# Four graph-attention layers on one core: the second half's destination tiles divided 5 + 3 instead of 6 + 2

## The chip, the core and the metric

The kernel runs on one NeuronCore of a Trainium2 chip. The metric is the device time of one execution in microseconds (us); the kernel is compared by the median of several executions. Engines are called by the profile's names: PE is TensorE (PEld its weight loads), DVE VectorE, ACT ScalarE, SP SyncE, POOL GpSimd.

## The reference

2048 nodes with 128 features each, in float32, pass through four layers `x = x + gnn(relu(layernorm(x)))` under one adjacency matrix. Layer 0 has eight heads; layers 1 to 3 have one. A head computes, for nodes n (destinations) and m (sources):

```
Wh = h @ W;   s1 = Wh @ a1;   s2 = Wh @ a2
e[n, m]  = leaky_relu(s1[n] + s2[m], 0.2), masked where adj[n, m] == 0
att      = softmax over m of e
out[n]   = act(att @ Wh)      # elu; exact gelu in layer 1; the heads of layer 0 are joined and go through W_out
```

## The kernel before

**Tiles and passes.** The 2048 nodes are 16 tiles of 128. The weights of the softmax are built transposed, 128 sources by up to 1024 destinations, by one VectorE instruction per source tile (`late_probs`, L1166; L1070 for the heads of layer 0 before the last half), and land in `probs`, a ring of eight slots of 1024 columns. TensorE takes them as stationary operand and multiplies them with `V` (129 columns: 128 features and one of factors, whose sum is the denominator), adding up over 16 source tiles in PSUM. One such matmul in float32 shows as two records. The destinations of a pass are `groups(p)`, each a group of 129 columns in `acc`; three groups fit a bank of 512.

The destinations of a layer are taken in three passes p = 0, 1, 2, numbered by `PARTS`: pass 0 has the first half (eight tiles), pass 1 six tiles of the second half, pass 2 the last two. In this text pass 1 is called the second pass and pass 2 the last pass. Each entry of `PARTS[p]` is a chunk of (first tile, count), in which the work behind a pass is done: denominators (`late_denominators`), division or activation from PSUM (`late_divide`, or `nonlinear_late` on ScalarE), ELU or GELU, the add to the node rows `X` (`add_linear`, `add_to_x`), statistics (`late_moments`, `late_variance`), inverse root (ScalarE's `late_inverse_root` and VectorE's `late_scale`; in layer 1's output for passes 0 and 1 Newton steps on VectorE alone), normalised rows (`late_norm` on VectorE, `late_normed` on ScalarE, shared out by `NORM_DVE`), transposes on TensorE (`transpose_normed`), ReLU into `hT` (`late_relu`, L834), and the next layer's `Wh` and scores (`late_wh`, L483). Layer 0 also has a transpose and a projection of its last head's rows (`transpose_rows`, `project_rows`).

**The seam.** A new layer can start its first pass only when the scores of all 16 tiles are there: `take_scores` reads the score columns from PSUM, the maximum over all of them is spread to all partitions by a matmul (`spread_late_max`, L497), `late_center` subtracts it, and `late_factors` and `exponent_rows` make the factors that the first `late_probs` needs.

**The order** on each engine is written out by hand, and an engine runs its instructions in that order, waiting on semaphores. On TensorE work of other kinds stands inside a pass at a place (j, half): behind the first half of the groups of source tile j (half 0), or behind all (half 1). In the layers' main sequence on VectorE (from L1363 on) the calls `tiles(n, p, first, end)` build source tiles; before, all sixteen of the last pass stand directly behind those of the second pass, and the second pass's denominators follow them. For the last pass four source tiles share one slot of the ring (256 columns each), and VectorE waits for a slot once for four. In layers 0 and 2 the last pass's `late_denominators` and `late_divide` stand, on VectorE, ahead of part of the second pass's work (`late_moments(1, 1)`; `late_norm(3, 1)`). On ScalarE `late_inverse_root` of the last pass stands ahead of the second pass's `late_relu` in layer 1 (both chunks) and in layer 2 (its second chunk).

Of the kernel before, what the change touches and what calls it, by code (L numbers as in the profile page):

```python
# [14 lines left out]
def gat_stack(nc, x, adj_t, w0, w0_t, a0, w_out, b_out, w1_t, w1, r1, w2, w2_t, av2, w3, w3_t, av3, out):  # L15
# [5 lines left out]
    N, D = x.shape  # L21
    H = w0.shape[0]
    P = 128
# [16 lines left out]
    PARTS = (((0, 4), (4, 4)), ((0, 4), (4, 2)), ((6, 2),))  # L40
    FIRST, CHUNKS = (0, 2, 4), 5
    NORM_DVE = ((0, 0), (1, 1), (2,))

    ctx = ExitStack()
    with ctx:
# [43 lines left out]
        late_part = sb("late_part", [P, 1])  # L89
# [24 lines left out]
        warm_bank, spare_bank, max_bank = acc[:, 1, 0, 0:P], acc[:, 0, 2, 0:2 * P], acc[:, 0, 2, 2 * P:3 * P]  # L114
# [96 lines left out]

        def group(c, k):

            return acc[:, c, k // PER_BANK, (k % PER_BANK) * VW:(k % PER_BANK) * VW + VW]
# [50 lines left out]
        def slot_no(n, p, j):  # L265

            return NT * (2 * H - 2) + (2 * NT + NT // 4) * n + NT * p + (j // 4 if p == 2 else j)
# [3 lines left out]
        def slot_of(n, p, j):  # L271

            at = (j % 4) * width(p) if p == 2 else 0
            return probs[:, slot_no(n, p, j) % RING, at:at + width(p)]
# [56 lines left out]
        def _(pe):  # L331
# [61 lines left out]
            def unit(u, c, q, asides=()):  # L393

                for j in range(NT):
# [10 lines left out]
                    for k in range(NK):  # L406
                        if first and k == NK // 2:
                            pe.wait_ge(probs_ready, 1)
                        last = nc.tensor.matmul(group(c, k), probs[:, j % RING, k * P:(k + 1) * P], V[:, j, :],  # L409
                                                start=(j == 0 and k % PER_BANK == 0), stop=(j == NT - 1),  # L410
# [6 lines left out]
            def late_unit(n, p, asides):  # L417

                c, v = half_of(p), V_of[n % 2]
                for j in range(NT):  # L420
# [8 lines left out]
                    for i, k in enumerate(groups(p)):  # L429
                        if p == 0 and j == 0 and k == NK // 2:  # L430
                            pe.wait_ge(probs_ready, tile_no(n, p, j) + 1)
                        last = nc.tensor.matmul(group(c, k), slot_of(n, p, j)[:, i * P:(i + 1) * P], v[:, j, :],  # L432
                                                start=(j == 0 and k % PER_BANK == 0), stop=(j == NT - 1),
# [134 lines left out]
            def rest_of_scores(n):  # L568
# [10 lines left out]
                else:  # L579
# [7 lines left out]
                late_s1(n, 2, hT_ready, chunk_no(n, 1, 0))  # L587
# [10 lines left out]
            late_unit(0, 2, {(9, 1): lambda: transpose_rows(1, 0, hT_ready, 1),  # L598
                             (10, 1): lambda: transpose_rows(1, 1, hT_ready, 2),
                             (11, 1): lambda: project_rows(1, 0),  # L600
                             (13, 0): lambda: project_rows(1, 1)})
# [368 lines left out]
        def _(dve):  # L970
# [54 lines left out]
            def last_columns(to, c):  # L1025

                full = NK // PER_BANK
                nc.vector.tensor_copy(to[:, 0:full * PER_BANK].rearrange("p (b g) -> p b g", g=PER_BANK),
                                      acc[:, c, 0:full, D:D + PER_BANK * VW - D:VW])
                link(nc.vector.tensor_copy(to[:, full * PER_BANK:NK],  # L1030
                                           acc[:, c, full, D:D + (NK - full * PER_BANK - 1) * VW + 1:VW]))
# [137 lines left out]
            def tiles(n, p, first, end):  # L1169

                for j in range(first, end):
# [4 lines left out]
                    if p < 2 or j % 4 == 0:  # L1176
# [11 lines left out]
            def late_denominators(n, p):  # L1188
# [3 lines left out]
                whole = 2 * PER_BANK  # L1192
# [326 lines left out]
```

## Time and profile before

| | |
|---|---|
| median of 3 runs | 776.5 us (775.86 to 779.19) |
| the profiled execution's own time | 776.41 us |
| its span (first to last instruction) | 774.7 us |
| mean granted TensorE clock | 0.988 of full speed |
| PE busy | 750.0 us (97%) |
| DVE busy | 626.4 us (81%) |
| ACT busy | 328.8 us (42%) |
| seam 1, layer 0 to 1: end of the last pass, first matmul of the next pass | 551.8 us, 567.8 us |
| seam 2, layer 1 to 2 | 627.9 us, 641.6 us |
| seam 3, layer 2 to 3 | 702.0 us, 712.6 us |
| end of the last pass of layer 3 | 770.5 us |

Times inside the execution are microseconds from the start of the span. A busy TensorE is counted from records whose ends are modelled, so the start of a record says more than its end. In the chain of work that ended last each piece was released by the one ahead of it; where the chain stays on one line of TensorE, nothing else holds the kernel up. In a timeline several instructions of a kind are merged into one row, with their number at the end and, in brackets, the idle time of the engine ahead of them.

### The profile page before, as it was taken

Reading aid. Unit: us, or ns where it says so; the run is one execution under the profiler, and the core shown is the slowest. Engines: PE = TensorE matmul, PEld = TensorE weight load, DVE = VectorE, ACT = ScalarE, POOL = GpSimd, SP = SyncE. Lnnn points to the kernel's source line nnn. Section 1 sums busy time; section 2 is a strip of 40 time slices with the busy share of each in tenths; the row PEclk is TensorE's granted clock in tenths of the full one; section 3 lists DMA queues with packets and bytes.
Section 4 is the critical chain, followed back from the end, with each engine's and each line's share of the span. In section 5 each row is a group of like instructions: output and inputs, shape, how many; then the busy total and the mean of one; then the engine's idle time right before and its main releaser. Section 6 shows DMA issues by size and latency. Waiting matters only on the chain.

```text
span 774.7 us, 15961 instructions
## 1 busy us (share of the span) xinstructions
PE 750.0 (97%) x6451; PEld 731.0 (94%) x6451; DVE 626.4 (81%) x1042; ACT 328.8 (42%) x888; POOL 16.1 (2%) x36
## 2 busy tenths in 40 slices
PE   8899899999999999999999999999889989998997
PEld 7699799999999999999999999999789969996997
DVE  4896788797877978879788796888588949997986
ACT  5875562343543246134354334623441244535420
POOL 3000000000000000000000000000000000000000
PEclk9999999999999999999999999999999989999999
DMA  9794000000000000000000000000000000000001
GB/s 298 269 364 159 28 2 28 27 0 27 2 25 27 0 27 0 27 27 0 27 17 10 27 0 27 0 0 2 0 2 1 1 1 1 2 1 1 1 19 38
DMA packets 13874, 29.39 MB, mean 38 GB/s; under 512 B 1296, under 2 KB 7568, under 8 KB 13840
## 3 DMA queue, kind: packets, MB, share of 16 engines
q1 hardware_dynamic: 11152, 20.00, 7.6%
q0 software_dynamic: 2688, 8.92, 3.4%
q8 instruction: 24, 0.39, 0.2%
q14 instruction: 10, 0.08, 0.0%
HBM read 27.80 MB, written 1.11 MB: 37 GB/s over the span
## 4 chain that ended last, share of the span: by engine, by line
PE 85%; ACT 5%; DMA 4%; DVE 4%; issue 1%; SPq 0%; DVEq 0%; ACTq 0%
PE acc L409 49%; PE acc L432 25%; DMA stage<-in_adj_t_dram 4%; PE side L509 3%; PE side L365 3%; PE acc L483 2%; ACT adjT L623 1%; DVE probs L1070 1%; ACT hpT L716 1%; DMA W0t<-in_W_t_dram 1%; PE side L471 1%; ACT hT L834 0%; PE side L457 0%; PE side L491 0%; ACT xn L825 0%
## 5 line engine op out<-in xcount | busy, mean ns | idle before, releaser
L409 PE MATMUL acc<-V,probs 128*128 128x129 f32 x3840 | 438.1, 276 | 1.9 <-DVE probs L1064 1.9
L409 PEld LDWEIGHTS acc<-V,probs 128*128 128x128 f32 x3840 | 434.0, 192 | 4.9 <-ACT V L657 2.7
L1070 DVE SCALAR_TENSOR_TENSOR probs<-rho,t_now,adjT 128x1024 f32<-128x1024 f32 x224 | 272.9, 1277 | 11.4 <-PE acc L409 9.1
L1166 DVE SCALAR_TENSOR_TENSOR probs<-rho,t_now,adjT 128x768 f32<-128x768 f32 (+3 forms) x179 | 146.7, 880 | 9.6 <-PE acc L432 6.6
L716 ACT ACTIVATE hpT<-rows 32x256 f32<-32x256 f32 x224 | 92.8, 414 | 71.1 <-DVE rows L1107 68.6
L432 PEld LDWEIGHTS acc<-stage,probs 128*128 128x128 f32 x1024 | 115.0, 192 | 4.0 <-ACT stage L865 3.7
L432 PE MATMUL acc<-stage,probs 128*128 128x129 f32 x1024 | 116.1, 275 | 2.1 <-DVE probs L1166 2.1
L432 PE MATMUL acc<-V,probs 128*128 128x129 f32 x768 | 89.4, 275 | 0.0
L432 PEld LDWEIGHTS acc<-V,probs 128*128 128x128 f32 x768 | 87.4, 192 | 1.0 <-ACT V L865 0.9
L1115 DVE TENSOR_TENSOR X<-X,side 128x512 f32<-128x512 f32 x28 | 19.3, 688 | 65.0 <-PE side L509 65.0
L701 ACT ACTIVATE fill<-mean_now,empty 128x128 f32<-128x128 f32 x112 | 34.2, 397 | 87.9 <-DVE den L1083 87.9
L679 ACT ACTIVATE V<-v_now 128x4 f32<-128x4 f32 x28 | 5.9, 209 | 82.2 <-PE side L365 82.2
L1092 DVE SCALAR_TENSOR_TENSOR rows<-acc,den,fill 128x128 f32<-128x128 f32 x112 | 30.9, 343 | 7.1 <-ACT fill L701 6.8
L623 ACT ACTIVATE adjT<-stage 128x1024 bf16<-128x1024 int32 x32 | 33.0, 1052 | 8.5 <-DMA stage<-in_adj_t_dram 8.4
L509 PE MATMUL side<-Wout,hpT 128*128 x224 | 28.9, 285 | 3.8 <-ACT hpT L716 3.8
L681 ACT ACTIVATE V<-side,v_now 128x128 f32<-128x128 f32 x112 | 31.4, 362 | 0.0
L509 PEld LDWEIGHTS side<-Wout,hpT 128*128 128x128 f32 x224 | 27.7, 202 | 4.0 <-issue 4.0
L365 PE MATMUL side<-W,hT 128*128 x224 | 29.6, 275 | 0.0
L365 PEld LDWEIGHTS side<-W,hT 128*128 128x128 f32 x224 | 27.3, 192 | 0.0
L800 ACT ACTIVATE rows<-acc,late_den 128x128 f32<-128x128 f32 x32 | 11.0, 398 | 36.4 <-DVE late_den L1203 21.6
L825 ACT ACTIVATE xn<-X,nwt 128x128 f32<-128x128 f32 x36 | 14.6, 481 | 18.5 <-DVE nwt L1304 18.5
L708 ACT ACTIVATE rows<-rows 128x512 f32<-128x512 f32 x28 | 17.7, 631 | 10.9 <-DVE rows L1092 10.7
(190 smaller groups left out, 416.6 us busy)
## 6 DMA issues: line engine op xcount, KB each, us to landing
stage<-in_adj_t_dram SPq DMA_DIRECT2D x32, 512.0 KB, 7.0
rho<-rho_dram POOLq DMA_DIRECT2D x15, 512.0 KB, 3.9
X<-in_x_dram SPq DMA_DIRECT2D x2, 512.0 KB, 4.4
W0t<-in_W_t_dram SPq DMA_DIRECT2D x1, 512.0 KB, 5.1
W<-in_L_gnn_W_heads_dram SPq DMA_DIRECT2D x1, 512.0 KB, 6.4
Wout<-in_L_gnn_W_out_dram POOLq DMA_DIRECT2D x1, 512.0 KB, 10.4
out_dram<-X SPq DMA_DIRECT2D x1, 512.0 KB, 3.7
out_dram<-X SPq DMA_DIRECT2D x1, 384.0 KB, 3.0
```

The costliest lines, as they stand in the source:

```text
L365: last = nc.tensor.matmul(side[:, g % 2, k * D:(k + 1) * D], hT[:, j * P:(j + 1) * P], w, start=True, stop=True)
L409: last = nc.tensor.matmul(group(c, k), probs[:, j % RING, k * P:(k + 1) * P], V[:, j, :], start=(j == 0 and k % PER_BANK == 0), stop=(j == ...
L432: last = nc.tensor.matmul(group(c, k), slot_of(n, p, j)[:, i * P:(i + 1) * P], v[:, j, :], start=(j == 0 and k % PER_BANK == 0), stop=(j = ...
L509: last = nc.tensor.matmul(side[:, b, k * D:(k + 1) * D], hpT[:, 4 * b + k, :], w, start=True, stop=True)
L623: nc.scalar.activation(adjT[:, j, c * CH:(c + 1) * CH], stage[:, n % STAGE, :], ACT.Sign).then_inc(adj_ready, 1)
L681: last = nc.scalar.activation(V[:, 4 * g + k, 0:D], side[:, g % 2, k * D:(k + 1) * D], ACT.Copy, scale=v_now[:, 4 * g + k:4 * g + k + 1])
L701: ins = nc.scalar.activation(fill[:, k, :], mean_now[:, :], ACT.Copy, scale=empty[:, c, k:k + 1])
L716: last = nc.scalar.activation(hpT[b:b + Q, :, a:a + Q], rows[a:a + Q, 1, :, b:b + Q], ACT.Copy)
L1070: nc.vector.scalar_tensor_tensor(probs[:, j % RING, :], rho[:, c * CH:(c + 1) * CH], t_now[:, j:j + 1], adjT[:, j, c * CH:(c + 1) * CH], A ...
L1092: ins = nc.vector.scalar_tensor_tensor(rows[:, 0, k, :], group(c, k)[:, 0:D], den[:, 3, k:k + 1], fill[:, k, :], ALU.mult, ALU.add)
L1115: nc.vector.tensor_tensor(at, at, side[:, b, :].rearrange("p (k d) -> p k d", k=4), ALU.add).then_inc(x_added, 1)
L1166: return nc.vector.scalar_tensor_tensor(slot_of(n, p, j)[:, first:end], rho[:, at + first:at + end], t_now[:, j:j + 1], adjT[:, j, at + fi ...
```

## The change

`PARTS` divides the second half 5 + 3 instead of 6 + 2: the second pass has tiles 0 to 4 in chunks of 3 and 2, the last pass tiles 5 to 7 in one chunk. The banks of the second half hold 3, 2 and 3 groups (`BANKS`, `place`, `last_of_bank`), so that each bank belongs to one pass. `spare_bank`, where the last pass's chunk is transposed, is three tiles wide. A slot of the ring holds two source tiles of the last pass (384 columns each) instead of four (`PER_SLOT`). VectorE builds source tiles 0 to 11 of the last pass ahead of the second pass's denominators and 12 to 15 behind them (and behind the divisions, where there are any). In layer 0's last pass, `transpose_rows` and `project_rows` stand at source tiles 6 to 9 instead of 9 to 13. `late_denominators`, `last_columns` and `take_scores` read the denominators or scores bank by bank; the maximum of the scores is one reduction over all 16 columns behind the last copy, where before a partial maximum was joined with the last two columns straight from PSUM. `NORM_DVE` gives all three of the last pass's normalised tiles to VectorE, as both were before.

```diff
@@ -37,9 +37,11 @@
     ALPHA, EPS = 0.2, 1e-5
-    PARTS = (((0, 4), (4, 4)), ((0, 4), (4, 2)), ((6, 2),))
+    PARTS = (((0, 4), (4, 4)), ((0, 3), (3, 2)), ((5, 3),))
+    BANKS = ((0, 3, 6, 8), (0, 3, 5, 8))
+    PER_SLOT = 2
     FIRST, CHUNKS = (0, 2, 4), 5
-    NORM_DVE = ((0, 0), (1, 1), (2,))
+    NORM_DVE = ((0, 0), (1, 1), (3,))
@@ -86,7 +88,6 @@
         late_max = sb("late_max", [P, 1])
-        late_part = sb("late_part", [P, 1])
@@ -111,7 +112,7 @@
         first_xn = [xn, rows[:, 0, :, :]]
-        warm_bank, spare_bank, max_bank = acc[:, 1, 0, 0:P], acc[:, 0, 2, 0:2 * P], acc[:, 0, 2, 2 * P:3 * P]
+        warm_bank, spare_bank, max_bank = acc[:, 1, 0, 0:P], acc[:, 0, 2, 0:3 * P], acc[:, 0, 2, 3 * P:4 * P]
@@ -209,9 +210,19 @@
+        def place(c, k):
+            b = max(b for b in range(NB) if BANKS[c][b] <= k)
+            return b, k - BANKS[c][b]
+        def last_of_bank(c, b):
+            return acc[:, c, b, D:D + (BANKS[c][b + 1] - BANKS[c][b] - 1) * VW + 1:VW]
-            return acc[:, c, k // PER_BANK, (k % PER_BANK) * VW:(k % PER_BANK) * VW + VW]
+            b, at = place(c, k)
+            return acc[:, c, b, at * VW:at * VW + VW]
@@ -264,13 +275,13 @@
-            return NT * (2 * H - 2) + (2 * NT + NT // 4) * n + NT * p + (j // 4 if p == 2 else j)
+            return NT * (2 * H - 2) + (2 * NT + NT // PER_SLOT) * n + NT * p + (j // PER_SLOT if p == 2 else j)
-            at = (j % 4) * width(p) if p == 2 else 0
+            at = (j % PER_SLOT) * width(p) if p == 2 else 0
@@ -407,7 +418,7 @@
                         last = nc.tensor.matmul(group(c, k), probs[:, j % RING, k * P:(k + 1) * P], V[:, j, :],
-                                                start=(j == 0 and k % PER_BANK == 0), stop=(j == NT - 1),
+                                                start=(j == 0 and place(c, k)[1] == 0), stop=(j == NT - 1),
@@ -430,7 +441,7 @@
                         last = nc.tensor.matmul(group(c, k), slot_of(n, p, j)[:, i * P:(i + 1) * P], v[:, j, :],
-                                                start=(j == 0 and k % PER_BANK == 0), stop=(j == NT - 1),
+                                                start=(j == 0 and place(c, k)[1] == 0), stop=(j == NT - 1),
@@ -584,7 +595,7 @@
                 spread_late_max(n)
-                late_s1(n, 2, hT_ready, chunk_no(n, 1, 0))
+                late_s1(n, 2, hT_ready, chunk_no(n, 1, 1))
@@ -595,10 +606,10 @@
                              **scores_of_half(1, 15)})
-            late_unit(0, 2, {(9, 1): lambda: transpose_rows(1, 0, hT_ready, 1),
-                             (10, 1): lambda: transpose_rows(1, 1, hT_ready, 2),
-                             (11, 1): lambda: project_rows(1, 0),
-                             (13, 0): lambda: project_rows(1, 1)})
+            late_unit(0, 2, {(6, 0): lambda: transpose_rows(1, 0, hT_ready, 1),
+                             (7, 0): lambda: transpose_rows(1, 1, hT_ready, 2),
+                             (8, 0): lambda: project_rows(1, 0),
+                             (9, 0): lambda: project_rows(1, 1)})
@@ -1024,11 +1035,14 @@
-                full = NK // PER_BANK
-                nc.vector.tensor_copy(to[:, 0:full * PER_BANK].rearrange("p (b g) -> p b g", g=PER_BANK),
-                                      acc[:, c, 0:full, D:D + PER_BANK * VW - D:VW])
-                link(nc.vector.tensor_copy(to[:, full * PER_BANK:NK],
-                                           acc[:, c, full, D:D + (NK - full * PER_BANK - 1) * VW + 1:VW]))
+                if c == 0:
+                    full = NK // PER_BANK
+                    nc.vector.tensor_copy(to[:, 0:full * PER_BANK].rearrange("p (b g) -> p b g", g=PER_BANK),
+                                          acc[:, c, 0:full, D:D + PER_BANK * VW - D:VW])
+                else:
+                    for b in range(2):
+                        nc.vector.tensor_copy(to[:, BANKS[1][b]:BANKS[1][b + 1]], last_of_bank(1, b))
+                link(nc.vector.tensor_copy(to[:, BANKS[c][2]:NK], last_of_bank(c, 2)))
@@ -1173,7 +1187,7 @@
                         dve.wait_ge(late_rho_ready, 4 * n)
-                    if p < 2 or j % 4 == 0:
+                    if p < 2 or j % PER_SLOT == 0:
@@ -1189,16 +1203,8 @@
                 dve.wait_ge(summed, tile_no(n - 1, p, NT))
-                whole = 2 * PER_BANK
-                steps_of = ([(0, whole)] if ks[0] == 0 else []) + ([(whole, NK)] if ks[-1] == NK - 1 else [])
-                for k0, k1 in steps_of:
-                    if k0 == 0:
-                        src = acc[:, c, 0:2, D:D + PER_BANK * VW - D:VW]
-                    else:
-                        src = acc[:, c, 2, D:D + (k1 - k0 - 1) * VW + 1:VW]
-                    to = late_den[:, c, 2 if n == 2 else 1, k0:k1]
-                    if k0 == 0:
-                        to = to.rearrange("p (b g) -> p b g", g=PER_BANK)
+                for b in (range(NB) if p == 0 else (0, 1) if p == 1 else (2,)):
+                    src, to = last_of_bank(c, b), late_den[:, c, 2 if n == 2 else 1, BANKS[c][b]:BANKS[c][b + 1]]
@@ -1316,20 +1322,16 @@
-                whole = 2 * PER_BANK
                 dve.wait_ge(late_wh_psum, stage_no(n, p))
-                if p == 1:
-                    link(nc.vector.tensor_copy(scores[:, NK:NK + whole].rearrange("p (b g) -> p b g", g=PER_BANK),
-                                               acc[:, 1, 0:2, D:D + PER_BANK * VW - D:VW]))
-                    link(nc.vector.tensor_reduce(late_part[:, :], scores[:, 0:NK + whole], AX.X, ALU.max))
-                else:
-                    nc.vector.scalar_tensor_tensor(late_max[:, :], acc[:, 1, 2, D:D + 1], acc[:, 1, 2, VW + D:VW + D + 1],
-                                                   late_part[:, :], ALU.max, ALU.max).then_inc(late_max_ready, 1)
-                    link(nc.vector.tensor_copy(scores[:, NK + whole:NT], acc[:, 1, 2, D:D + (NK - whole - 1) * VW + 1:VW]))
+                for b in ((0, 1) if p == 1 else (2,)):
+                    last = nc.vector.tensor_copy(scores[:, NK + BANKS[1][b]:NK + BANKS[1][b + 1]], last_of_bank(1, b))
+                link(last)
+                if p == 2:
+                    nc.vector.tensor_reduce(late_max[:, :], scores[:, :], AX.X, ALU.max).then_inc(late_max_ready, 1)
@@ -1372,10 +1374,11 @@
             tiles(0, 1, 14, 16)
-            tiles(0, 2, 0, 16)
+            tiles(0, 2, 0, 12)
             late_divide(1, 1, 1)
+            tiles(0, 2, 12, 16)
@@ -1422,8 +1425,9 @@
                     tiles(1, 1, 13, 16)
-                    tiles(1, 2, 0, 16)
+                    tiles(1, 2, 0, 12)
                     late_denominators(2, 1)
+                    tiles(1, 2, 12, 16)
@@ -1446,10 +1450,11 @@
                     tiles(2, 1, 15, 16)
-                    tiles(2, 2, 0, 16)
+                    tiles(2, 2, 0, 12)
                     late_divide(3, 1, 1)
+                    tiles(2, 2, 12, 16)
@@ -1473,10 +1478,11 @@
                     tiles(3, 1, 14, 16)
-                    tiles(3, 2, 0, 16)
+                    tiles(3, 2, 0, 12)
                     late_divide(4, 1, 1)
+                    tiles(3, 2, 12, 16)
```

## Rows read from the trace of the kernel before

**Rows 1.** The page, the chain that ended last: shares of the span by line.

```profile
PE acc L409 49%; PE acc L432 25%; DMA stage<-in_adj_t_dram 4%; PE side L509 3%; PE side L365 3%; PE acc L483 2%; ACT adjT L623 1%; DVE probs L1070 1%; ACT hpT L716 1%; DMA W0t<-in_W_t_dram 1%; PE side L471 1%; ACT hT L834 0%; PE side L457 0%; PE side L491 0%; ACT xn L825 0%
```

**Rows 2.** The chain by time (start, us, what, records), layer 2, last pass.

```profile
694.83 7.15 PE acc L432 x64
```

**Rows 3.** The timeline (start, us, engine, line, operation, shapes, count): VectorE's passes.

```profile
533.20 8.27 DVE L1166 SCALAR_TENSOR_TENSOR probs<-rho,t_now,adjT 128x768 f32<-128x768 f32 x18
...
685.52 7.35 DVE L1166 SCALAR_TENSOR_TENSOR probs<-rho,t_now,adjT 128x768 f32<-128x768 f32 x17
```

**Rows 4.** The timeline, layer 0: second pass and last pass.

```profile
528.66 0.69 DVE L1255 TENSOR_TENSOR X<-X,side 128x512 f32<-128x512 f32 x1 [0.88 <-PE side L457]
...
533.31 3.19 ACT L825 ACTIVATE xn<-X,nwt 128x128 f32<-128x128 f32 x8 [1.04 <-DVE nwt L1304]
...
536.50 0.60 PE L471 MATMUL side<-ident,xn 128*128 128x128 f32 x4
...
541.82 0.17 DVE L1205 TENSOR_SCALAR late_den<-acc 128x6 f32<-128x6 f32 x1 [0.34 <-PE acc L432]
...
542.24 1.64 DVE L1221 SCALAR_TENSOR_TENSOR rows<-acc,late_den,fill 128x128 f32<-128x128 f32 x6
...
544.87 0.69 DVE L1231 SCALAR_TENSOR_TENSOR rows<-rows 128x512 f32<-128x512 f32 x1
...
546.97 0.60 PE L449 MATMUL side<-ident,rows 128*128 128x128 f32 x4
```

**Rows 5.** The timeline, seam between layers 0 and 1.

```profile
552.25 0.61 DVE L1221 SCALAR_TENSOR_TENSOR rows<-acc,late_den,fill 128x128 f32<-128x128 f32 x2
...
552.77 1.25 DVE L1269 BATCH_NORM_STATS2 stats<-X 128x6 f32<-128x128 f32 x6
...
560.08 0.29 ACT L811 ACTIVATE nwt<-mv,eps_col 128x2 f32<-128x2 f32 x1
...
562.49 0.38 PE L471 MATMUL acc<-ident,xn 128*128 128x128 f32 x2
...
564.55 0.49 PE L497 MATMUL acc<-ident,late_max 128*128 128x128 f32 x2 [0.40 <-DVE late_max L1330]
```

**Rows 6.** The timeline, second pass of layer 2: normalised rows and their transposes.

```profile
685.64 3.19 ACT L825 ACTIVATE xn<-X,nwt 128x128 f32<-128x128 f32 x8 [1.97 <-DVE nwt L1304]
...
688.66 0.60 PE L471 MATMUL side<-ident,xn 128*128 128x128 f32 x4
```

**Rows 7.** The timeline, seam between layers 1 and 2.

```profile
630.07 0.60 ACT L800 ACTIVATE rows<-acc,late_den 128x128 f32<-128x128 f32 x2
...
632.42 0.58 ACT L834 ACTIVATE hT<-side 128x512 f32<-128x512 f32 x1
...
635.09 0.63 PE L471 MATMUL acc<-ident,xn 128*128 128x128 f32 x2
...
637.91 0.80 PE L497 MATMUL acc<-ident,late_max 128*128 128x128 f32 x2 [0.40 <-DVE late_max L1330]
```

**Rows 8.** The timeline, seam between layers 2 and 3.

```profile
703.60 0.60 DVE L1313 TENSOR_SCALAR xn<-X,mv,nwt 128x128 f32<-128x128 f32 x2
...
705.37 0.29 ACT L811 ACTIVATE nwt<-mv,eps_col 128x2 f32<-128x2 f32 x1
...
709.36 0.49 PE L497 MATMUL acc<-ident,late_max 128*128 128x128 f32 x2 [0.40 <-DVE late_max L1330]
```

**Rows 9.** Windows: stretch, length, busy us by engine (PE first), PEclk, DMA, GB/s.

```profile
557.00:559.00 2.00, 0.54 (x5) 0.57 (x6) 1.59 (x8) 1.65 (x4) 0.00 (x0) 0.98 0.00 0
...
559.00:561.00 2.00, 1.65 (x8) 1.25 (x7) 0.32 (x2) 1.44 (x6) 0.00 (x0) 0.50 0.00 0
...
634.00:636.00 2.00, 1.72 (x9) 1.32 (x7) 0.33 (x2) 0.24 (x1) 0.00 (x0) 0.51 0.00 0
```

**Rows 10.** DMA issues: count, KB each, us from issue to landing.

```profile
out_dram<-X SPq DMA_DIRECT2D x1, 384.0 KB, 3.0
...
out_dram<-X SPq DMA_DIRECT2D x1, 128.0 KB, 1.8
```

## The prediction

> **What bounds the kernel now.** The first view is the page's chain of work that ended last, by line: the two matmul lines of the attention passes (L409, L432) carry 49% and 25% of the span [rows 1]. TensorE is therefore the bound wherever passes run, and the change leaves the number of matmuls as it is. The second view is the same chain in order of time, from 515 us on: inside a pass it is a single run of L432, the last pass of a layer being 64 matmul records in 7.15 us, 0.1117 us each [rows 2], two records for one fp32 matmul, so 0.223 us for one tile of destinations. Between the last matmul of a layer and the first of the next the chain breaks into small pieces on VectorE, ScalarE and TensorE: three seams (their bounds stand in the table of the profile) and a tail. So I read the timeline there, asking for each seam which of two strands ends last: the one of the second pass (destinations 8 and up) or that of the last pass.
>
> **The passes.** Per source tile the second pass takes five matmuls instead of six and the last pass three instead of two: 16 x (5+3) is 16 x (6+2). TensorE's sum is unchanged, but the second pass ends 16 x 0.223 = 3.57 us earlier. For VectorE the two longest runs of L1166 differ by one 768-wide instruction, 8.27 - 7.35 = 0.92 us; the rest of the shorter run is sixteen 256-wide ones, 6.43 us, 0.402 each [rows 3]. The line through both (0.518 us for 512 columns) is 0.14 us + 1.01 ns per column: 0.79 us for 640 columns, 0.53 us for 384. I take that slope for every other instruction that gets wider too: +0.13 us for 128 columns. Sum per source tile 1.32 us as before. The ring is what shifts: two last-pass tiles share a slot now instead of four, so the last four wait for tiles 14 and 15 of the second pass, and stand behind the second pass's denominators and divisions. They start at the latest 2 us after the second pass's end and TensorE wants tile 12 only 12 x 0.67 = 8 us into the last pass: no cost for TensorE, but 4 x 0.53 = 2.1 us more ahead of everything that VectorE does next for the second pass.
>
> **Where TensorE may now stand inside a pass.** TensorE gets earlier by 0.22 us per second-pass tile, VectorE by only 0.13, so work that TensorE takes from the other engines in mid-pass loses slack.
> - Layer 0, second pass. The add to X behind the projection at tile 7 (528.66) comes 8 x 0.223 = 1.79 us earlier, one 768-wide tile then saves 0.13: the normalised rows of ScalarE are 1.92 us earlier. TensorE wants them at tile 13, 14 x 0.223 = 3.13 us earlier. Of eight instructions in 3.19 us four are done after 1.65, so ready was 533.31+1.65+0.14 (semaphore) = 535.10 against 536.50 [rows 4]: slack 1.40 goes to 0.19. No cost.
> - Layer 0, last pass. VectorE is through with its asides at 533.20-1.92 = 531.28; two tiles and twelve of the last pass (1.58+6.38) end at 539.24, while the second pass, whose denominators began at 541.82, ends 3.57 earlier, at 538.2. Denominators 0.42, five divisions at 0.26 (six and two of them take 1.64 and 0.61, [rows 4, 5]), four tiles 2.1 and the first ELU (0.4+0.55 at 384 columns) make its rows ready at 544.15 with the semaphore; before they were at 545.56 with TensorE there at 546.97 [rows 4]. The transposes stood behind ten tiles, so the last pass began at 546.97 - 10x0.447 = 542.50, and now begins at 538.93; their new place, inside tile 6 behind one of three, comes at 538.93 + 6x0.67 + 0.22 = 543.17. TensorE stands 1.0 us. The second chunk (tile 7) is then in time. One tile less in this transposing and projecting gives 0.33 back: the pass ends 0.65 later.
> - Layer 2, second pass. By the same count the normalised rows are 1.04 + 3 x 0.13 = 1.43 us earlier (VectorE's tile 11 starts when second-pass tile 3 is done, four tiles of 0.22, and is itself 0.13 shorter), TensorE 3.13 us: 685.64+1.65+0.14 = 687.43 against 688.66 [rows 6] is slack 1.23, and becomes -0.47. Cost **0.5 us**.
> - Layers 1 and 3: no such point ends late by this count.
>
> **Seam 1 (layer 0 to 1).** Here VectorE keeps its order: denominators of the last pass, its divisions, and only then the statistics of the second pass. So its strand starts with the last matmul and the 3.57 us of cover buy nothing. The divisions gain one (+0.26), the ELU and its transposes are wider (+0.2, +0.1, copy +0.1); one statistic less is -0.2 (six took 1.25). ScalarE's root of the last part (560.08) is queued behind the copy of the transposed second-pass rows: with 0.65 from the pass I put it at 560.70. The add to X, statistics and norm of three instead of two (+0.13, +0.26, +0.26) overlap with that wait but for the norm: ready for TensorE at 562.8. Before, the transposes began at 562.49, and it was TensorE that was late, coming from a stretch with a clock of 0.50 [rows 5, 9]. Transpose +0.11, relu +0.11, two matmul records more +0.22, scores +0.15 (copy and then maximum, where one instruction of 0.22 did both): the spread of the maximum (564.55, [rows 5]) comes at 565.5. **+1.0 us**, the wait in the pass included.
>
> **Seam 2.** The one seam where the second pass's strand is late: its statistics and the Newton steps end only after the last matmul, so ScalarE comes to the last pass's GELU at 630.07 and, past a table load and the root, to the second pass's relu at 632.42 [rows 7]. With 3.57 us more cover, less the 2.1 us of tiles, this strand is out of the way, and the GELU starts on the last denominators, 0.4 us behind the last matmul, at 628.35. From GELU to relu took 2.35 us; a third tile adds 0.6 (division or GELU 0.26, add 0.07 to 0.13, statistics 0.26): relu at 631.3, 1.1 earlier. From here the clock decides. It was 0.51 in 634 to 636 [rows 9], and the transposes at 635.09 waited for TensorE's own slow matmuls. If it stays at 2.4 GHz, the norm sets them, at 633.0, and 2.06 for the way to the spread with 0.6 for the third tile gives 635.7 instead of 637.91, with 0.3 more behind it: -2.5. If it falls before 632, the third tile eats the gain: -0.2. From transpose to spread took 2.82 at the low and 2.06 at the high clock [rows 5, 7]. I take **-1.5**, a little nearer to the fast end, since TensorE's idle stretch ahead of the relu shrinks by that 1.1 us.
>
> **Seam 3.** The second pass's strand was ready before the last matmul except for VectorE's two norms (703.60), which stand behind denominators, divisions and an add of the last pass, and they stay there. VectorE is one serial chain: +0.26 division, +0.13 and +0.13 for two adds to X, +0.26 statistics, so the root at 705.37 moves to 706.15; norm +0.26, transpose and relu +0.22, matmuls +0.22, scores +0.15 up to the spread (709.36) [rows 8]. **+1.6 us.** The second chunk's relu waits behind that root on ScalarE, inside the same stretch. Nothing is late next.
>
> **Tail.** Division and two adds of 384 columns: +0.5; the last store is 192 KB instead of 128: between 1.8 and 3.0 us for 128 and 384 KB [rows 10], +0.3. **+0.8 us.** Two more copies of last columns per denominator lie under TensorE's passes; where VectorE sets a wait they add 0.1 in all.
>
> **Sum.** 1.0 + 0.5 - 1.5 + 1.6 + 0.8 + 0.1 = +2.5 us on the profiled execution (776.41 us, span 774.7), which is the median of 776.5 to 0.1. So **779.0 us**, +0.3%. About 0.5% (3.9 us) is what a measurement of this kernel can tell from no change.
>
> **Rivals.**
> - *The cover works everywhere.* VectorE is ahead enough that TensorE doesn't stand in the passes (-0.5, and seam 1 without its 1.0), and seam 2 brings its full 2.5: 1.6+0.8+0.1-2.5 = 0.0, 776.5 us. For it: slacks of 0.2 to 1 us rest on a straight line between two widths. Against: two separate waits would have to be absent.
> - *The clock, slower.* In seam 3 TensorE's holes grow: behind the first three second-pass matmuls about 0.9 us, behind the last two 0.7, where before it had nearly none. Before seam 1's drop its busy time was 0.54 of 2 us [rows 9]; I count about 0.8 to 1.0 of 2 here. If it falls, transpose to spread is 0.76 longer [rows 5, 7] and the second-pass matmuls some 0.4; with seam 2 at -0.2 the sum is 1.0+0.5-0.2+1.6+0.8+0.1+1.2 = +5.0, 781.5 us. It decides if the granted clock is at its low level anywhere in the first 9 us of seam 3. The Trainium skill (TensorE: Matmul & The Clock Gate, "What's actually happening") says that the throttled state is the default and activity releases it; by that rule a seam that grew idler is the place to fall. This trace agrees in two seams of three.
> - *The cover is not used in seam 2 either* (another engine's order holds it): 1.0+0.5+1.6+0.8+0.1 = +4.0, 780.5 us.
>
> **Chances.** Forecast 0.40, cover everywhere 0.25, cover unused 0.11, clock 0.17, a gain I don't see 0.07. Slower by over 0.5%: the clock and half of the unused cover, 0.23; faster 0.07; within 0.70. The range takes in 776.5 and 781.5 with the few tenths by which executions differ: 775.8 to 781.9.
>
> **What would show it.** In the profile after: layer 0's transposes in the last pass with some 1 us of idle TensorE before them; VectorE's last four tiles right behind the divisions; GELU of the last part at about 0.4 us behind the last matmul in seam 2, relu some 1 us earlier; in seam 3 the root 0.8 us further behind the last pass's denominators; a tail 0.8 us longer. The forecast is wrong if seam 3 is not longer, or if seam 2's gain is not near 1 to 2 us.

## Result, and the profile after

The changed kernel takes 779.36 us (median of 20 runs, 777.66 to 781.76), the kernel before 776.88 (20 runs, 773.91 to 779.19); the ratio is 1.0033, 95% interval 1.0022 to 1.0044. The medians differ by 2.5 us (2.6 by the ratio), which is below the 0.5% that was called no change, and clear of zero. The profiled execution of the changed kernel took 777.76 us, near the fastest of its twenty.

The page of the kernel after: its span, TensorE's busy time and the chain by line. Line numbers are 11 higher on TensorE and ScalarE: L443 is L432 of before, L482 is L471, L494 L483, L502 L491, L508 L497, L811 L800, L822 L811, L836 L825, L845 L834.

```profile
span 776.1 us, 15973 instructions
...
PE 749.7 (97%) x6451; PEld 730.7 (94%) x6451; DVE 627.5 (81%) x1060; ACT 328.1 (42%) x885; POOL 16.1 (2%) x36
...
PE acc L420 50%; PE acc L443 23%; DMA stage<-in_adj_t_dram 4%; PE side L520 3%; PE side L376 3%; DVE probs L1180 2%; PE acc L494 1%; ACT adjT L634 1%; PE acc L390 1%; ACT hpT L727 1%; DVE stats L1275 1%; DVE rows L1227 0%; PE side L502 0%; ACT hT L845 0%; PE side L468 0%
```

TensorE is busy for 749.7 us instead of 750.0: the work is the same, and the chain has lost 2% at the pass line (L443 23%, L432 25% [rows 1]) to VectorE (L1180, L1275, L1227). That share is the length of the chain on VectorE ahead of two points where TensorE now waits for it, in layer 0 and in layer 2; it is not the length of the waits. To see how long they are, I cut both profiled executions at TensorE's own marks: the first matmul of layer 0's second pass, the first score matmul behind each last pass (L491, now L502), and the matmul for the mean (L389, now L400), which stands inside the first pass of layers 2 and 3.

| stretch, us | before | after | difference | forecast |
|---|---|---|---|---|
| layer 0, second and last pass | 36.58 | 37.30 | +0.72 | +0.65 |
| seam 1 and layer 1 | 76.28 | 76.76 | +0.48 | +0.35 |
| seam 2 to the mean of layer 2 | 28.12 | 25.65 | -2.47 | -1.5 |
| layer 2 to the end of its last pass | 45.77 | 46.27 | +0.50 | +0.5 |
| seam 3 to the mean of layer 3 | 25.37 | 27.18 | +1.81 | +1.6 |
| layer 3 and the tail | 47.55 | 48.32 | +0.77 | +0.8 |
| sum | 259.67 | 261.48 | +1.81 | +2.5 (0.1 for the copies in it) |

(The heads of layer 0 ahead of this took 0.46 us less in the execution after, 514.61 us against 515.07; more of that below. Where times of layer 0 and seam 1 are compared with those of before, these 0.46 us have to be added.)

Layer 0, the timeline after (start us, us, engine, line, operation, shapes, count, idle before and its end):

```profile
538.75 0.22 DVE L1211 TENSOR_SCALAR late_den<-acc 128x3 f32<-128x3 f32 x2
...
540.54 2.20 DVE L1180 SCALAR_TENSOR_TENSOR probs<-rho,t_now,adjT 128x384 f32<-128x384 f32 x4
...
543.04 0.56 DVE L1237 SCALAR_TENSOR_TENSOR rows<-rows 128x384 f32<-128x384 f32 x1
...
543.75 0.52 PE L460 MATMUL side<-ident,rows 128*128 128x128 f32 x3 [0.87 <-DVE rows L1237]
...
560.22 0.29 ACT L822 ACTIVATE nwt<-mv,eps_col 128x3 f32<-128x3 f32 x1
...
562.38 0.85 PE L482 MATMUL acc<-ident,xn 128*128 128x128 f32 x3
...
565.37 0.49 PE L508 MATMUL acc<-ident,late_max 128*128 128x128 f32 x2 [0.53 <-DVE late_max L1334]
```

The second pass's denominators come at 538.75, three microseconds ahead of 541.82 [rows 4] (2.6 when the earlier start is taken off); the last four tiles (540.54) stand behind the divisions, the ELU behind them, and TensorE waits 0.87 us for it at 543.75. In seam 1 the last part's transposes begin at 562.38 and the spread comes at 565.37. With the 0.46 us added that is 562.84 and 565.83, 0.35 and 1.28 us later than before [rows 5] (forecast: 562.8 and 565.5). TensorE's clock falls in this seam as it did before: the three transposes take 0.85 us, where e5, whose clock stays high, takes 0.52 for them, starts them the same 10.5 us behind the pass's end, and reaches the spread 0.33 us sooner. In the window 560 to 562 the granted clock is at its low level:

```profile
560.00:562.00 2.00, 1.98 (x9) 1.98 (x10) 1.11 (x6) 0.72 (x4) 0.00 (x0) 0.50 0.00 0
```

Seam 2, the timeline, and two windows of it (columns as in [rows 9], the granted clock third from the right):

```profile
629.09 0.88 ACT L811 ACTIVATE rows<-acc,late_den 128x128 f32<-128x128 f32 x3 [2.75 <-DVE late_den L1209]
...
632.10 0.47 ACT L845 ACTIVATE hT<-side 128x384 f32<-128x384 f32 x1
...
633.93 0.49 PE L482 MATMUL acc<-ident,xn 128*128 128x128 f32 x3
...
636.56 0.49 PE L508 MATMUL acc<-ident,late_max 128*128 128x128 f32 x2 [0.53 <-DVE late_max L1334]
```

```profile
633.00:635.00 2.00, 1.43 (x13) 1.19 (x12) 0.91 (x5) 1.05 (x5) 0.00 (x0) 1.00 0.01 4
...
635.00:637.00 2.00, 1.38 (x9) 1.19 (x10) 0.33 (x2) 0.53 (x2) 0.00 (x0) 1.00 0.00 0
```

The last pass ends at 628.67 here, at 627.93 before. Counted from there, the last part's GELU starts after 0.4 us where it was 2.1; the relu comes after 3.4 us, 4.5 before [rows 7]; the clock stays at its high level, where it was 0.51 [rows 9].

Layer 2's second pass, seam 3 and the tail, the timeline; then a window behind the spread of seam 3, and the last store (count, KB, us to landing):

```profile
682.48 3.19 ACT L836 ACTIVATE xn<-X,nwt 128x128 f32<-128x128 f32 x8 [1.70 <-DVE nwt L1310]
...
684.27 0.63 PE L482 MATMUL side<-ident,xn 128*128 128x128 f32 x4 [0.31 <-ACT xn L836]
...
702.77 0.60 DVE L1319 TENSOR_SCALAR xn<-X,mv,nwt 128x128 f32<-128x128 f32 x2
...
704.94 0.30 ACT L822 ACTIVATE nwt<-mv,eps_col 128x3 f32<-128x3 f32 x1 [0.58 <-DVE mv L1281]
...
709.75 0.72 PE L508 MATMUL acc<-ident,late_max 128*128 128x128 f32 x2 [0.53 <-DVE late_max L1334]
...
771.08 0.16 DVE L1211 TENSOR_SCALAR late_den<-acc 128x3 f32<-128x3 f32 x1 [4.88 <-PE acc L443]
```

```profile
711.00:713.00 2.00, 2.00 (x4) 0.67 (x2) 1.59 (x4) 1.83 (x7) 0.00 (x0) 0.50 0.00 0
```

```profile
out_dram<-X SPq DMA_DIRECT2D x1, 192.0 KB, 2.1
```

TensorE waits for ScalarE's normalised rows at 684.27, which is 1.65 + 0.14 us behind their start, as counted for before [rows 6]. In seam 3 the last pass's denominators come at 700.79; before, they came at 702.02, and those of the tail at 770.49:

```profile
702.02 0.16 DVE L1205 TENSOR_SCALAR late_den<-acc 128x2 f32<-128x2 f32 x1 [0.64 <-PE acc L432]
...
770.49 0.16 DVE L1205 TENSOR_SCALAR late_den<-acc 128x2 f32<-128x2 f32 x1 [2.96 <-PE acc L432]
```

From these denominators to the root it is 4.15 us instead of 3.35 [rows 8], to the spread 8.96 instead of 7.34. In seam 3 the clock falls only about the spread (0.50 in 711 to 713). From the denominators to the end of the span the tail takes 5.0 us instead of 4.2.

### The profile page after: what moved, and what is told of

It is laid out like the page before. It is cut to its first block, busy times and chain, and to the rows that moved or that the text cites. A ratio compares the mean times of both kernels' runs of the same rounds, so it can differ in the third digit from the quotient of the medians.

```text
span 776.1 us, 15973 instructions
## 1 busy us (share of the span) xinstructions
PE 749.7 (97%) x6451; PEld 730.7 (94%) x6451; DVE 627.5 (81%) x1060; ACT 328.1 (42%) x885; POOL 16.1 (2%) x36
## 4 chain that ended last, share of the span: by engine, by line
PE 84%; DVE 7%; ACT 4%; DMA 4%; issue 1%; POOL 0%; DVEq 0%; ACTq 0%; POOLq 0%
PE acc L420 50%; PE acc L443 23%; DMA stage<-in_adj_t_dram 4%; PE side L520 3%; PE side L376 3%; DVE probs L1180 2%; PE acc L494 1%; ACT adjT L634 1%; PE acc L390 1%; ACT hpT L727 1%; DVE stats L1275 1%; DVE rows L1227 0%; PE side L502 0%; ACT hT L845 0%; PE side L468 0%
## 5 line engine op out<-in xcount | busy, mean ns | idle before, releaser
L1180 DVE SCALAR_TENSOR_TENSOR probs<-rho,t_now,adjT 128x640 f32<-128x640 f32 (+3 forms) x179 | 146.9, 878 | 12.3 <-PE acc L443 8.4
L443 PEld LDWEIGHTS acc<-stage,probs 128*128 128x128 f32 x1024 | 115.1, 192 | 2.8 <-ACT stage L876 2.6
L443 PE MATMUL acc<-stage,probs 128*128 128x129 f32 x1024 | 115.8, 275 | 1.0 <-DVE probs L1180 1.0
L443 PE MATMUL acc<-V,probs 128*128 128x129 f32 x768 | 89.4, 275 | 1.0 <-DVE probs L1180 1.0
L443 PEld LDWEIGHTS acc<-V,probs 128*128 128x128 f32 x768 | 87.4, 192 | 1.9 <-ACT V L876 1.8
L811 ACT ACTIVATE rows<-acc,late_den 128x128 f32<-128x128 f32 x32 | 11.1, 398 | 39.0 <-DVE late_den L1209 24.2
L719 ACT ACTIVATE rows<-rows 128x512 f32<-128x512 f32 x28 | 17.7, 630 | 10.6 <-DVE rows L1106 10.5
L836 ACT ACTIVATE xn<-X,nwt 128x128 f32<-128x128 f32 x33 | 13.5, 482 | 16.8 <-DVE nwt L1310 16.8
```

Of the source, the lines that this page charges most:

```text
L1180: return nc.vector.scalar_tensor_tensor(slot_of(n, p, j)[:, first:end], rho[:, at + first:at + end], t_now[:, j:j + 1], adjT[:, j, at + fi ...
```

## Experiments

Each is compared with the kernel before on the same chip in 10 to 12 runs, and by its profile with the same marks as above. A profile shows a stretch to 0.1 us; the ratios of the medians don't, their intervals are 0.3 to 0.4% wide. e5 to e8 ran on another chip than e1 to e4, so only ratios and stretches are compared between the two groups.

### e1: layer 0's asides two source tiles later

```diff
-            late_unit(0, 2, {(6, 0): transpose_rows(1, 0, ..), (7, 0): transpose_rows(1, 1, ..),
-                             (8, 0): project_rows(1, 0), (9, 0): project_rows(1, 1)})
+            late_unit(0, 2, {(8, 0): transpose_rows(1, 0, ..), (9, 0): transpose_rows(1, 1, ..),
+                             (10, 0): project_rows(1, 0), (11, 0): project_rows(1, 1)})
```

> The changed kernel with the four asides of layer 0's last pass (transposes and projection of the second pass's rows) two source tiles later: tiles 8, 9, 10 and 11 instead of 6, 7, 8 and 9. My theory: TensorE waits 0.87 us at tile 6 for VectorE's ELU, because VectorE comes to the second pass's denominators late and builds four more tiles first; two tiles later (1.34 us) the rows are there. Expected: no idle TensorE ahead of the transposes, the last pass of layer 0 ends 0.9 us earlier, the adds to X still well before it ends, the rest unchanged: 0.9 us less than the changed kernel, ratio to the kernel before about 1.002. Rival, the wait is no loss since TensorE waits elsewhere for it: the last pass ends at the same time, ratio 1.003.

Measured: 777.16 us, ratio 1.0017 (1.0003 to 1.0032). Layer 0's two passes take 36.25 us, 1.05 less than in the changed kernel and even 0.33 less than before, as forecast from the one tile that is projected behind the pass instead of in it. The transposes, in e1's timeline, have no idle time before them:

```profile
543.52 0.56 DVE L1237 SCALAR_TENSOR_TENSOR rows<-rows 128x384 f32<-128x384 f32 x1
...
544.52 0.49 PE L460 MATMUL side<-ident,rows 128*128 128x128 f32 x3
```

Seam 1 and layer 1 stay as they were (76.67 against 76.76). So the wait was a real loss of TensorE's time, and it depends on where the asides stand in the pass: with the same split, two source tiles later it is gone.

### e2: the second pass's strand ahead of the last pass's denominators

```diff
+            late_statistics(1, 1)
+            late_scale(1, 1)
+            late_norm(1, 1)
             late_denominators(1, 2)
             late_divide(1, 2, 0)
-            late_moments(1, 1)
             late_elu_rows(2, 0)
-            late_variance(1, 1)
-            late_scale(1, 1)
-            late_norm(1, 1)
...
+                    late_norm(3, 1)
                     late_denominators(3, 2)
                     late_divide(3, 2, 0)
                     add_linear(3, 2, 0)
-                    late_norm(3, 1)
```

and on ScalarE `late_inverse_root(1, 1)` and `late_normed(1, 1)` ahead of `late_exp_rows(1, 2, 0)`, and the second part of `late_normed(3, 1)` ahead of `late_exp_rows(3, 2, 0)`.

> The changed kernel with the second pass's strand taken out from behind the last pass's denominators where it stood behind them. In layer 0 statistics, scale and norm of the second pass stand ahead of the last pass's denominators on VectorE, and root and normalised rows ahead of the last pass's exponentials on ScalarE; in layer 2 the two norms of the second pass stand ahead of the last pass's denominators. My theory, the longer cover was bought and left unused there by the order: from the end of the last pass to the spread of the maximum seam 1 shrinks by about 1.7 us and seam 3 by 0.5; in all 2.2 us less than the changed kernel, ratio about 1.000 to 1.001. Rival, the strand of the last pass alone (its ELU, projection, statistics, norm) binds both seams whatever stands beside it: less than 0.5 us in all, ratio 1.003.

Measured: 777.95 us, ratio 1.0028 (1.0009 to 1.0047), where 1.000 to 1.001 was expected; the median does not tell e2 from the changed kernel. Past layer 0's heads its profile takes 260.40 us, 1.1 less than the changed kernel's 261.48 and not the 2.2 expected. From the end of the last pass to the spread, seam 1 is 1.04 us shorter (12.42 against 13.46), seam 3 0.51 (8.65 against 9.16). Seam 1 fell short of 1.7 for a reason its own timeline shows:

```profile
561.18 0.52 PE L482 MATMUL acc<-ident,xn 128*128 128x128 f32 x3 [1.47 <-DVE xn L1318]
...
562.37 1.66 PE L494 MATMUL acc<-WL,hT 128*128 128x129 f32 x6 [0.67 <-ACT hT L845]
...
564.55 0.79 PE L508 MATMUL acc<-ident,late_max 128*128 128x128 f32 x2 [0.53 <-DVE late_max L1333]
...
565.14 3.62 PE L502 MATMUL side<-hT,waL 128*128 128x512 f32 x4
```

The transposes came 1.4 us sooner behind the pass's end (9.05 us against 10.47). But TensorE, through with the second pass's work earlier, idled 1.47 us ahead of them. In the changed kernel the clock had fallen with the second pass's matmuls and was high again at the spread; now it fell behind the transposes and stayed low past the spread (0.50 in 566 to 568): six records that take 0.94 took 1.66, the four behind the spread 3.62 instead of 1.88. Of the 1.04 us at the spread only 0.2 are left at the next layer's first matmul. So VectorE's order did hold the cover back, as the theory has it; the clock took most of that gain again in seam 1.

### e3: the same order with 6 + 2

The diff is that of e2, on the kernel before.

> The kernel before (6 + 2) with the same change of order as in e2. My theory: with 6 + 2 the second pass's strand in layer 0 is not finished when the last pass ends (its last add to X ends 0.7 us ahead of the end), so putting it first delays the last pass's denominators by about 3 us and takes about as much out of the strand behind them: seam 1 within 1 us of the kernel before, either way; in seam 3 the two norms (0.5 us) fit ahead of the end: seam 3 shorter by 0.4. Ratio 0.999 to 1.001. Rival, the order alone is worth as much without the new split: ratio 0.997, as far below the kernel before as e2 is below the changed kernel.

Measured: 776.57 us, ratio 1.001 (0.999 to 1.0029). Seam 1 and layer 1 take 76.51 us (+0.23), seam 3 24.85 to the mean (-0.52). A row of its timeline, whose last pass ends at 551.97: the last pass's denominators, which came 0.2 us behind the pass in the kernel before, now wait for the second pass's statistics and norm.

```profile
555.11 0.15 DVE L1204 TENSOR_SCALAR late_den<-acc 128x2 f32<-128x2 f32 x1
```

The denominators come 3 us later, as expected, and seam 1 does not gain. In layer 0 the order needs the longer cover of 5 + 3; in seam 3 it does not.

### e4: seam 2 of the kernel before, with TensorE kept active

```diff
                     transpose_normed(n, 1, 1, hT_ready, chunk_no(n, 0, 1))
+                    if n == 2:
+                        keep_warm(9, warm_bank)
```

> The kernel before with nine matmuls of the identity on TensorE in seam 2, between the transposes of the second pass and the matmuls for the scores, where TensorE idles 2.4 us. They hold nothing up; they keep TensorE active. It measures what part of seam 2's gain in the changed kernel (2.5 us in the two profiles) is the clock and what the earlier relu. My theory: the clock stays at its high level; the transposes of the last pass come 0.6 us earlier, the spread 1.1 us earlier, the first matmul of layer 2's passes 1.2 to 1.5 us earlier: ratio 0.998 to 0.9985. Rival, the gain is all from the relu and the clock is a by-product: under 0.3 us, ratio 1.000.

Measured: 774.66 us, ratio 0.9984 (0.9966 to 1.0002), which by itself is not clear of no change. Seam 2 to the mean takes 26.53 us instead of 28.12: -1.59. The granted clock is 1.00 from 628 to 634 and 634 to 636.

```profile
628.06 2.17 PE L379 MATMUL acc<-ident 128*128 128x128 f32 x18
...
630.60 1.61 PE L483 MATMUL acc<-WL,hT 128*128 128x129 f32 x12 [0.36 <-ACT hT L836]
...
634.09 0.49 PE L497 MATMUL acc<-ident,late_max 128*128 128x128 f32 x2 [0.39 <-DVE late_max L1332]
```

The nine matmuls (628.06) end before the relu lets the others begin (630.60). So of the 2.47 us that seam 2 gains in the changed kernel 1.6 are the clock and 0.9 the earlier relu, less the third tile. (e5 and e6 below, both with a high clock there, differ by the same 0.9.)

### e5 and e6: both splits with the seams kept active

Matmuls of the identity as in e4: in e5, the changed kernel, 5 behind `project_rows(2, 0)`, 7 in seam 2, 3 and 2 around the second chunk's `late_wh` in seam 3; in e6, the kernel before, 6 and 9 in seams 1 and 2. Both kernels already have four such matmuls early in seam 1; these come on top.

> The changed kernel with matmuls of the identity in TensorE's idle stretches of all three seams (5, 7 and 3+2), nothing else. Executions of the changed kernel between 777.66 and 781.76 us go with mean granted clocks from 0.992 down to 0.984. My theory: what differs between them is in which seams the clock falls; kept active, TensorE stays at its high level, the executions lie within 2 us of each other and the median is 1.5 to 2 us lower than the changed kernel's: ratio to the kernel before 1.001 to 1.0015. Rival, the spread has another source (the projections, the first heads, the memory): the spread stays near 4 us and the median moves by under 0.5 us, ratio 1.003.

> The kernel before with matmuls of the identity in seams 1 and 2 (6 and 9); seam 3 has no idle stretch over 0.4 us. Beside e5 it gives the change's effect with the clock out of it. My theory: seam 1 +1.2 (the wait in layer 0's last pass in it), seam 2 -0.9, layer 2's second pass +0.5, seam 3 +1.8, tail +0.8 and the split's seam 1 without the cold stretch of before +0.3: the changed kernel with warm seams is 3.3 to 3.7 us slower than this one, which is itself 1.6 to 2.2 us faster than the kernel before: ratio 0.9975. Rival, the clock treats both splits alike: e5 and e6 differ by the same 2.5 us as the kernels without.

Measured: e5 778.97 us, ratio 1.0027 (1.0011 to 1.0043); e6 772.89 us, ratio 0.9961 (0.9942 to 0.9981), and 2.08 us less than the kernel before past the heads, as expected. e5's expectation failed and its rival held: executions still lie between 776.14 and 780.29 us, though the mean granted clock is 0.992 to 0.995 in all of them. So most of the spread is not made in the seams; the last section has a part of its source. Past layer 0's heads, where the profiles can be compared, e5 takes 260.91 us and e6 257.58: 3.3 apart, at the lower edge of the 3.3 to 3.7 that the terms gave and not the rival's 2.5. By stretch: +0.74, +0.64, -0.90, +0.51, +1.56, +0.78. With the clock out of it the split costs 3.3 us by these profiles; in the plain kernels seam 2's clock gives 1.6 of that back. The medians are 6.1 us apart. In the two profiled executions the heads, which both kernels do with the same matmuls, account for 2.1 of the rest (515.30 us in e5, 513.23 in e6); what else the medians hold is not shown.

### e7 and e8: the edits together, and the best of 6 + 2

e7 is the changed kernel with e1, e2 and

```diff
-                    tiles(2, 1, 13, 15)
+                    tiles(2, 1, 13, 14)
                     late_scale(3, 0)
-                    tiles(2, 1, 15, 16)
+                    tiles(2, 1, 14, 16)
...
                     late_relu(3, 1, 0)
-                    late_inverse_root(3, 2)
                     late_relu(3, 1, 1)
+                    late_inverse_root(3, 2)
```

and matmuls of the identity (7 in seam 2, 5 ahead of the last part's transposes in the others). e8 is e6 with `late_norm(3, 1)` and ScalarE's share moved as in e2.

> The changed kernel with e1's asides and e2's order, VectorE's scale of layer 2's first half one source tile earlier (against the 0.5 us that TensorE waits in that pass), the second chunk's relu in seam 3 ahead of the last part's root, and matmuls of the identity in the idle stretches of the seams. My theory, by the terms measured one by one against the changed kernel: layer 0's last pass -1.0, seam 1 -1.7 with the clock held, layer 2's pass -0.5, seam 3 -0.7, the clock -1: 4.5 to 5 us less than the changed kernel, ratio to the kernel before 0.997, level with e6. Rival, the waits replace each other (the next late engine stands 0.5 us behind in each place): no more than 2.5 us less than the changed kernel, ratio 1.000.

> e6 (6 + 2, warm seams) with the two norms of layer 2's second pass ahead of the last pass's denominators. In e3 that edit took 0.5 us out of seam 3 of the kernel before. It asks whether 5 + 3 is needed for that gain. My theory: no, the 6 + 2 strand is ready 0.6 us ahead of the end of the pass, and this is 0.5 us faster than e6: ratio 0.997. If the norms delay the denominators instead, level with e6.

Measured: e7 774.85 us, ratio 0.9981 (0.9964 to 0.9998); e8 774.65 us, ratio 0.997 (0.9956 to 0.9984). Past the heads e7 takes 258.09 us, 3.4 less than the changed kernel, e8 257.06. e7 by stretch against the changed kernel: -1.06, -1.08, 0.0, -0.50, -0.76, 0.0. Its expectation of 4.5 to 5 failed, and so did its rival's 2.5. Of the missing 1.5 us, 1.0 was a term for the clock that seam 1's term already held. The other 0.6 is missing in seam 1, by a wait of the kind that the rival named: with e1's later asides the second pass's rows are added later, and in e2's order its norm, which starts at 549.54, then holds the last pass's denominators back to 550.05, 0.9 us behind the pass's end at 549.17 where e2 has 0.2. e8 met its expectation by the profile (0.5 us less than e6, all of it in seam 3); by the medians it did not, with 774.65 us against e6's 772.89. The spread in seam 3, behind denominators at the same 0.2 us from the pass's end, shows what stays:

```profile
696.28 1.88 PE L502 MATMUL acc<-hT,waL 128*128 128x512 f32 x4
...
704.93 0.49 PE L508 MATMUL acc<-ident,late_max 128*128 128x128 f32 x2 [0.53 <-DVE late_max L1337]
```

```profile
699.63 1.88 PE L491 MATMUL acc<-hT,waL 128*128 128x512 f32 x4
...
706.65 0.49 PE L497 MATMUL acc<-ident,late_max 128*128 128x128 f32 x2 [0.40 <-DVE late_max L1332]
```

8.65 us with three tiles in the last pass, 7.02 with two: the third tile's 1.6 us, with everything else out of the way. In seam 1 both take 12.4. All three of e6, e7 and e8 are faster than the kernel before, by 1.5 to 3 us by the ratios; their medians don't tell them apart, and by their profiles 5 + 3 is 1.0 us behind 6 + 2 at its best.

## Why the prediction was right

The forecast was 779.0 us (+2.5); the runs gave 779.36 (+2.6 by the ratio), and the signs and places of all terms held. That the total agrees this well is in part luck: the forecast was made of such stretches, and in the two profiles they add up to +1.8 us and not to +2.5, with one term off by 1.0. Point by point:

- **Wait in layer 0's last pass**: forecast 1.0 us at the transposes, found 0.87 in the timeline; shown by e1, which took it away and made the stretch 1.05 us shorter.
- **Seam 1**: with the wait forecast +1.0, found +1.20 by the two first stretches. The unused cover was the step on which this rested, and e2 showed it: with the order changed the transposes come 1.4 us sooner. From transposes to spread the forecast had 2.7 us and the profile 2.99; in e5, with a high clock, it is 2.66, so the excess is the clock.
- **Seam 2**: the mechanism held (relu forecast 1.1 us earlier, found 1.06), the term was mis-sized: -1.5 forecast, -2.47 found, which is outside the 1 to 2 us that the prediction itself had set as its test for this seam. The step was the choice between the two ends for the clock, -0.2 and -2.5; it stayed high in the three profiles of 5 + 3 without added matmuls (the changed kernel, e1, e2) and fell in both such profiles of 6 + 2 with nothing added in this seam (before, e3). The fast end was the right one. e4 gives the clock's share, 1.6.
- **Layer 2**: forecast +0.5, found +0.50; e7's earlier scale removed it.
- **Seam 3**: forecast +1.6, found +1.62 at the spread and +1.81 at the mean, the 0.2 being the clock behind it. The rival's fall of the clock did occur in this profile (and in e1's, not in e2's), but at the spread, where it costs 0.2 and not 1.2; it neither came inside the stretch that the rival named nor at its price. It was close: the clock is low from about 709.9 on, 9.3 us into the seam, and the rival had named the first 9. The holes of TensorE that the rival counted as 0.9 and 0.7 us measured 0.54 and 0.50.
- **Tail**: forecast and found +0.8.

The six terms of the pair of profiles add up to 1.81 us, the medians differ by 2.5. What fills the 0.7 is not settled: an execution's clock and start differ from one to the next by more than that, and only one of each is profiled. The mean granted clock of the changed kernel's twenty executions goes from 0.982 to 0.992, with 0.990 in the profiled one, so a further fall of the clock in the slower ones is possible; none of those was profiled.

## What to carry to other kernels

A longer cover for one strand pays only where that strand ends last and nothing of it is queued behind the other strand's first wait: look for both before moving the split, and count the work added to the strand that is left uncovered, instruction by instruction. Where an engine gets earlier inside a pass, list each point at which it takes something from another engine, with its slack; that list gave the two waits here to some 0.1 us. And a gain in a gap of TensorE can be a gain of its clock: some matmuls of the identity in the gap of the old kernel tell the two apart. Here they gained 2.1 us by the profile of e6, where the change itself lost time.

## What the runs showed that I had not expected

**Much of the spread of the executions is made before 120 us.** Between out-projections of layer 0 every profile takes 32.16 us per pair of passes from the second one on; but the second began at 118.43 us before, at 117.97 after, at 115.86 in e4 and at 116.59 in e6. One part is the clock: in the stretch from 70 to 116 us its mean is 0.96 in the kernel before and 1.00 in e4, which have the same code there, and the chain by time shows the first out-projection's 16 records. The kernel before, window and chain, then e4, window and chain:

```profile
70.00:116.00 46.00, 42.23 (x365) 42.04 (x364) 39.93 (x53) 23.61 (x67) 0.53 (x1) 0.96 0.03 13
```

```profile
84.63 3.60 PE side L509 x16
```

```profile
70.00:116.00 46.00, 43.53 (x390) 43.34 (x389) 38.94 (x49) 23.41 (x66) 1.06 (x2) 1.00 0.06 20
```

```profile
83.97 1.67 PE side L509 x15
```

(In e4 the first of the 16 records starts at 83.60; all 16 take 2.05.) TensorE had waited for the first head's rows ahead of both; whether its clock is low behind that wait is worth some 1.5 us. The other part is how long the adjacency takes to load: the last piece of its load in the chain ends at 67.4 us in the kernel before, at 68.7 in e2, and the out-projection begins 17.2 us behind it in both; in the ten profiles it began between 83.60 and 85.93 us. Together they make 2.9 us between the earliest and the latest of the ten at the second out-projection, as much as the change itself, out of the 5.3 us by which the executions of the kernel before differ, which is why the stretches and not the medians settle the experiments.

**Clearing TensorE's queue early can cost its clock.** In e2 the second pass's matmuls were done sooner, an idle stretch of 1.47 us stood behind them, and the low clock that followed took back 0.8 of the 1.04 us gained at the spread. e7 has the same order with that stretch filled, and its clock stays high. The Trainium skill (TensorE: Matmul & The Clock Gate, "What's actually happening") has activity as what releases the throttle; the runs agree: the granted clock is 1.00 through both seams 1 and 2 in the profiles of e5 to e8, where identity matmuls filled the gaps of both, while in e4, which fills seam 2 alone, it still fell in seam 1.
